# Two loads of chunk 0 become one load in two partition halves, and nine warm-up products become eight

## The chip, the cores and the metric

The kernel runs on one core of one Trainium2 chip. The metric is device time in microseconds (us) of one execution, lower is better. The engines named below are TensorE (PE in rows; its weight loads are PEld), VectorE (DVE), ScalarE (ACT), GpSimd (POOL) and SyncE (SP). Each has its own queue of instructions and waits on semaphores for the others. SP and ACT each also issue DMA transfers on a queue of their own.

## What is computed

A residual layer over 2048 tokens with 512 features: a base projection, and a low-rank addition gated by the two best of eight experts.

```python
base = jnp.einsum('btd,od->bto', x, W)
logits = jnp.einsum('btd,ed->bte', x, Wr) + bias[:, None, :]   # 5.0 at the language's expert
topw, topi = jax.lax.top_k(logits, 2)
gates = jnp.sum(jax.nn.one_hot(topi, E) * jax.nn.softmax(topw)[..., None], axis=-2)
h = jnp.einsum('btd,erd->bter', x, A)
lora_out = jnp.einsum('bter,bte,eor->bto', h, gates, B)
return x + base + 2.0 * lora_out
```

## The kernel before

The 2048 tokens are 16 tiles of 128. The 512 features are four chunks (`k` 0 to 3) of 128, which are the contraction of one product. All weights stand side by side in 648 columns: 392 head columns (`heads_cols`: the second half of W, A and Wr) and 256 base columns (`base_cols`: the first half of W). To keep float32 accuracy in fast products, each operand is split into an upper part (`x_hi`, `w_hi`, a rounded copy) and a lower part (`x_lo`, `w_lo`, what is left), and three products stand for one: hi by hi, hi by lo, lo by hi.

Tiles 0 and 1 come with the weights in one array, `first`, laid out by chunk: 256 columns of x, 4 of language ids, 392 head columns, 256 base columns, 908 in all, on 128 partitions. Before the change they arrive as follows. SP issues x and ids of chunk 0 (L165, semaphore `x_landed`), the base columns of chunk 0 (L166, `wb_landed`), whole chunks 2 and 3 (L168), then tile 2, B and the groups of later tiles. ACT issues the head columns of chunk 0 (L253, `wh_landed`), then whole chunk 1 (L254, `chunk_landed[0]`).

When x has landed, ACT makes `x_hi` of chunk 0 for both tiles (L232), and POOL `x_lo` from it (L211). When the head columns have landed, DVE makes their `w_hi` (L362, `wh_hi_made`), then their `w_lo` (L358). When the base columns have landed, ACT makes their `w_hi` (L235, `w_hi_made`), and DVE their `w_lo`. ACT then goes on with chunk 1.

PE begins with `warm(WARM_UP)`, nine products of ones of 128x512 into a bank that nothing reads (L502). Then, for tiles 0 and 1 of chunk 0 (L429): two head products hi by hi, which wait for `x_hi` and the head columns' `w_hi`; two base products hi by hi, which wait for the base columns' `w_hi`; four products with `x_lo`; two head and two base products with `w_lo`. Chunks 1 to 3 follow in the same manner, then tile 2, and from tile 3 on one step a tile, with the low-rank products of the tile before (L469, L473) and the transposition of its gated heads (L460) in between. No order is planned by a table: it is the order of the code on each engine.

```python
            warm(WARM_UP)
            pe.wait_ge(chunk_hi_made, 1)
            pe.wait_ge(wh_hi_made, 1)
            for t in FIRST:
                heads_product(t, 0, 0)
            pe.wait_ge(w_hi_made, 1)
            for t in FIRST:
                base_product(t, 0, 0)
```

Of the kernel before, what the change touches and what calls it, by code (L numbers as in the profile page):

```python
# [12 lines left out]
P = 128  # L13
# [10 lines left out]
HEADS = REST + ER + E  # L24
SLOTS = 3
LANG_BIAS = 5.0
SCALING = 2.0
WARM_UP = 9
WIDTH = HEADS + BASE


# [1 line left out]
FIRST_X = len(FIRST) * P  # L33
IDS = 4
# [4 lines left out]
def cond_resid_program(nc: bass.Bass, first: bass.AP, xT: bass.AP, x: bass.AP,  # L39
# [11 lines left out]
    with ctx:  # L51
        def sb(name, shape, dt=FP32):
            return ctx.enter_context(nc.sbuf_tensor(name, shape, dt))
# [4 lines left out]
        def sem(name):  # L58
            return ctx.enter_context(nc.semaphore(name))


        first_sb = sb("first_sb", [P, KC, FIRST_X + IDS + WIDTH])
# [31 lines left out]
        warm_ps = ps("warm_ps")  # L94


        x_landed = sem("x_landed")
        xT_third = sem("xT_third")
        xT_group = sem("xT_group")
        x_group = sem("x_group")  # L100
        xT_last = sem("xT_last")
        x_last = sem("x_last")
        wh_landed = sem("wh_landed")
        wb_landed = sem("wb_landed")
        chunk_landed = [sem(f"chunk_landed{k}") for k in range(1, KC)]
        b_landed = sem("b_landed")
# [37 lines left out]
        heads_cols, base_cols, all_cols = slice(0, HEADS), slice(HEADS, WIDTH), slice(0, WIDTH)  # L144
# [4 lines left out]
        w_sb = first_sb[:, :, FIRST_X + IDS:]  # L149
        w = first[:, :, FIRST_X + IDS:]  # L150

        block = ctx.enter_context(nc.Block())

        @block.sync
        def _(sp):
            def load(dst, src, t, n, landed):
                sp.dma_start(dst[:, bass.ds(t, n), :], src[:, bass.ds(t, n), :]).then_inc(landed, 16)

            def store(t, n):
                sp.dma_start(out[:, bass.ds(t, n), :], out_sb[:, bass.ds(t, n), :]).then_inc(out_stored, 16)  # L160

            def load_xT(t, n, landed):
                load(xT_sb, xT, t - len(FIRST), n, landed)

            sp.dma_start(first_sb[:, 0, 0:FIRST_X + IDS], first[:, 0, 0:FIRST_X + IDS]).then_inc(x_landed, 16)  # L165
            sp.dma_start(w_sb[:, 0, base_cols], w[:, 0, base_cols]).then_inc(wb_landed, 16)  # L166
            for k in range(2, KC):
                sp.dma_start(first_sb[:, k, :], first[:, k, :]).then_inc(chunk_landed[k - 1], 16)  # L168
            load_xT(2, 1, xT_third)
            sp.dma_start(b_sb[:, :], b).then_inc(b_landed, 16)  # L170

            load_xT(3, SLOTS, xT_group)
            load(x_sb, x, 0, SLOTS, x_group)
            with sp.Fori(0, GROUPS - 2) as g:
                sp.wait_ge(xT_group, 16 * g + 16)
                sp.wait_ge(x_group, 16 * g + 16)
                load_xT(SLOTS * g + 3 + SLOTS, SLOTS, xT_group)
                load(x_sb, x, SLOTS * g + SLOTS, SLOTS, x_group)
            sp.wait_ge(x_group, 16 * (GROUPS - 1))
            load(x_sb, x, GROUPED - SLOTS, SLOTS, x_group)  # L180
            load_xT(GROUPED, TILES - GROUPED, xT_last)
            load(x_sb, x, GROUPED, TILES - GROUPED, x_last)
            with sp.Fori(0, GROUPS) as g:
                sp.wait_ge(out_made, SLOTS * g + SLOTS)
                store(SLOTS * g, SLOTS)
            for t in range(GROUPED, TILES - 2):
                sp.wait_ge(out_made, t + 1)
                store(t, 1)

            for t in range(TILES - 2, TILES):  # L190
                sp.wait_ge(heads_read, t + 1)
                sp.dma_start(out[:, t, BASE:O], out_sb[:, t, BASE:O]).then_inc(out_stored, 16)
                sp.wait_ge(out_made, t + 1)
                sp.dma_start(out[:, t, 0:BASE], out_sb[:, t, 0:BASE]).then_inc(out_stored, 16)
            sp.wait_ge(out_stored, 16 * (GROUPS + TILES - 2 - GROUPED + 4))
# [33 lines left out]
        @block.scalar  # L229
        def _(act):  # L230
            def chunk_upper(k):
                nc.scalar.activation(x_hi[:, 0:2, chunks[k]], first_x[k], ACT.Copy).then_inc(chunk_hi_made, 1)  # L232

            def w_upper(k, cols):
                nc.scalar.activation(w_hi[:, k, cols], w_sb[:, k, cols], ACT.Copy).then_inc(w_hi_made, 1)  # L235

            def x_upper(t, s, landed, count):

                act.wait_ge(landed, count)
                if not (isinstance(t, int) and t < SLOTS):  # L240
                    act.wait_ge(base_done, t - SLOTS + 1)
                nc.scalar.activation(x_hi[:, s, :], xT_sb[:, t - len(FIRST), :], ACT.Copy).then_inc(x_hi_made, 1)  # L242

            def ghT_upper(t, s, src=ghT_ps):
                act.wait_ge(transposed, t + 1)
                nc.scalar.activation(ghT_hi[s][:, :], src[:, 0:P], ACT.Copy).then_inc(ghT_hi_made, 1)  # L246

            def exponential(t):
                act.wait_ge(top_made, t + 1)
                nc.scalar.activation(e2[:, :], top[:, 0:1], ACT.Exp, scale=-1.0,  # L250
                                     bias=top[:, 1:2]).then_inc(e2_made, 1)

            act.dma_start(w_sb[:, 0, heads_cols], w[:, 0, heads_cols]).then_inc(wh_landed, 16)  # L253
            act.dma_start(first_sb[:, 1, :], first[:, 1, :]).then_inc(chunk_landed[0], 16)  # L254
            act.wait_ge(x_landed, 16)
            chunk_upper(0)
            act.wait_ge(wb_landed, 16)
            w_upper(0, base_cols)
            for k in range(1, KC):
                act.wait_ge(chunk_landed[k - 1], 16)  # L260
                chunk_upper(k)
                w_upper(k, base_cols if k == 1 else all_cols)
            x_upper(2, 2, xT_third, 16)
            act.wait_ge(b_landed, 16)
            nc.scalar.activation(b_hi[:, :], b_sb[:, :], ACT.Copy).then_inc(b_hi_made, 1)
            exponential(0)

            def step(t, j, landed, count):

                x_upper(t + 1, (j + 1) % SLOTS, landed, count)  # L270
                ghT_upper(t - 1, (j - 1) % SLOTS)
                exponential(t)

            exponential(1)
            ghT_upper(0, 0)
            with act.Fori(0, GROUPS - 1) as g:
                for j in range(2, 2 + SLOTS):
                    step(SLOTS * g + j, j, xT_group, 16 * g + 16)
            for t in range(GROUPED - 1, TILES - 1):
                step(t, t, xT_last, 16)  # L280
            last = TILES - 1
            act.wait_ge(x_last, 16)
            act.wait_ge(out_made, last - SLOTS + 1)
            nc.scalar.activation(base_ps[last % SLOTS][:, 0:BASE], x_sb[:, last, 0:BASE],
                                 ACT.Copy).then_inc(last_x_placed, 1)
            exponential(last)
            ghT_upper(last - 1, (last - 1) % SLOTS)
            ghT_upper(last, last % SLOTS, warm_ps)

        @block.vector  # L290
        def _(dve):
# [69 lines left out]
            def heads_upper(k):  # L361
                nc.vector.tensor_copy(w_hi[:, k, heads_cols], w_sb[:, k, heads_cols]).then_inc(wh_hi_made, 1)  # L362

            dve.wait_ge(wh_landed, 16)
            heads_upper(0)
            dve.wait_ge(wh_hi_made, 1)
            w_lower(0, heads_cols)
            dve.wait_ge(w_hi_made, 1)
            w_lower(0, base_cols)
            dve.wait_ge(expert_made, 1)  # L370
            dve.wait_ge(x_landed, 16)
            nc.vector.tensor_scalar(bias[:, :], expert[:, :], ids_sb, LANG_BIAS, ALU.is_equal,
                                    ALU.mult).then_inc(bias_made, 1)
            dve.wait_ge(chunk_landed[0], 16)
# [49 lines left out]
        def _(pe):  # L424
# [75 lines left out]
            def warm(times):  # L500
                for _ in range(times):
                    nc.tensor.matmul(warm_ps[:, :], ones, ones_moving, start=True, stop=True)  # L502

            warm(WARM_UP)
            pe.wait_ge(chunk_hi_made, 1)
# [122 lines left out]
```

## Time and profile before

| | us |
|---|---|
| median of three runs | 80.04 (79.7 to 80.2) |
| the profiled execution's own time | 79.61 |
| its span | 77.8 |

| engine | busy us | share of the span |
|---|---|---|
| PE | 74.0 | 95% |
| PEld | 70.3 | 90% |
| DVE | 48.9 | 63% |
| POOL | 22.6 | 29% |
| ACT | 22.4 | 29% |

A span runs from the first to the last instruction that the profile shows; 79.61 - 77.8 = 1.8 us of the profiled execution lie around it. Busy time of PE counts each product with its modelled end, so that products overlap, and a busy PE is not one at its peak: the distance from one start to the next is the better measure of a product's price. A DMA has two times: that of its issue on a queue, and that of its landing, which is when an engine that waits for it can go on.

### The profile page before, as it was taken

Reading aid. Unit: us, or ns where it says so; the run is one execution under the profiler, and the core shown is the slowest. Engines: PE = TensorE matmul, PEld = TensorE weight load, DVE = VectorE, ACT = ScalarE, POOL = GpSimd, SP = SyncE. Lnnn points to the kernel's source line nnn. Section 1 sums busy time; section 2 is a strip of 40 time slices with the busy share of each in tenths; the row PEclk is TensorE's granted clock in tenths of the full one; section 3 lists DMA queues with packets and bytes.
Section 4 is the critical chain, followed back from the end, with each engine's and each line's share of the span. In section 5 each row is a group of like instructions: output and inputs, shape, how many; then the busy total and the mean of one; then the engine's idle time right before and its main releaser. Section 6 shows DMA issues by size and latency. Waiting matters only on the chain.

```text
span 77.8 us, 1631 instructions
## 1 busy us (share of the span) xinstructions
PE 74.0 (95%) x505; PEld 70.3 (90%) x505; DVE 48.9 (63%) x220; ACT 22.4 (29%) x57; POOL 22.6 (29%) x26
## 2 busy tenths in 40 slices
PE   5979999999999999999999999999999999999960
PEld 2349999899999999999999999999999999999950
DVE  0098958879854829283755739283855739787750
ACT  1647901523503314140504113140404023122100
POOL 4039542055160505123060605123060606000000
PEclk9999999999999999999999999999999999999999
DMA  0999991795597399989900000450000072032143
GB/s 10 308 406 401 419 430 60 167 420 230 83 417 313 54 365 440 383 241 402 388 25 0 0 0 0 177 227 0 0 0 0 0 297 107 0 135 95 44 139 135
DMA packets 3893, 14.24 MB, mean 183 GB/s; under 512 B 432, under 2 KB 1328, under 8 KB 3632
## 3 DMA queue, kind: packets, MB, share of 16 engines
q1 hardware_dynamic: 3600, 13.52, 46.8%
q10 hardware_dynamic: 288, 0.67, 2.2%
q8 instruction: 2, 0.03, 0.2%
q14 instruction: 3, 0.02, 0.1%
HBM read 9.99 MB, written 4.19 MB: 182 GB/s over the span
## 4 chain that ended last, share of the span: by engine, by line
PE 90%; DMA 5%; DVE 1%; ACT 1%; SPq 0%; issue 0%
PE heads_ps L429 43%; PE base_ps L429 28%; PE heads_ps L469 5%; PE base_ps L469 5%; DMA first_sb<-in_first 5%; PE base_ps L473 2%; PE heads_ps L473 2%; PE ghT_ps L460 2%; PE base_ps L453 2%; DVE out_sb L421 1%; ACT w_hi L235 1%; SPq L165 0%; PE warm_ps L460 0%
## 5 line engine op out<-in xcount | busy, mean ns | idle before, releaser
L207 POOL TENSOR_TENSOR x_lo<-xT_sb,x_hi 128x512 fp32r<-128x512 f32 x14 | 18.1, 1294 | 39.0 <-ACT x_hi L242 37.2
L429 PE MATMUL heads_ps<-w_hi,x_hi 128*128 128x392 f32 x64 | 22.2, 357 | 0.0
L429 PE MATMUL heads_ps<-w_hi,x_lo 128*128 128x392 f32 x64 | 21.1, 342 | 0.0
L429 PE MATMUL heads_ps<-w_lo,x_hi 128*128 128x392 f32 x64 | 21.1, 340 | 0.0
L429 PE MATMUL base_ps<-w_hi,x_hi 128*128 128x256 f32 x60 | 16.5, 285 | 0.4 <-ACT w_hi L235 0.4
L429 PE MATMUL base_ps<-w_hi,x_lo 128*128 128x256 f32 x60 | 16.7, 281 | 0.0
L429 PE MATMUL base_ps<-w_lo,x_hi 128*128 128x256 f32 x60 | 16.3, 281 | 0.0
L294 DVE TENSOR_TENSOR ghT_lo<-ghT_ps,ghT_hi 128x128 fp32r<-128x128 f32 x15 | 4.3, 290 | 14.9 <-ACT ghT_hi L246 14.8
L246 ACT ACTIVATE ghT_hi<-ghT_ps 128x128 fp32r<-128x128 f32 x15 | 4.1, 275 | 29.5 <-PE ghT_ps L460 29.5
L429 PEld LDWEIGHTS heads_ps<-w_hi,x_hi 128*128 128x128 f32 x64 | 11.7, 188 | 0.9 <-ACT x_hi L232 0.5
L429 PEld LDWEIGHTS base_ps<-w_hi,x_hi 128*128 128x128 f32 x60 | 11.2, 188 | 0.8 <-ACT w_hi L235 0.8
L429 PEld LDWEIGHTS heads_ps<-w_lo,x_hi 128*128 128x128 f32 x64 | 11.9, 189 | 0.0
L429 PEld LDWEIGHTS heads_ps<-w_hi,x_lo 128*128 128x128 f32 x64 | 11.8, 188 | 0.0
L429 PEld LDWEIGHTS base_ps<-w_lo,x_hi 128*128 128x128 f32 x60 | 11.3, 189 | 0.0
L429 PEld LDWEIGHTS base_ps<-w_hi,x_lo 128*128 128x128 f32 x60 | 11.3, 188 | 0.0
L250 ACT ACTIVATE e<-top 128x1 f32<-128x1 f32 x16 | 4.7, 297 | 15.9 <-DVE top L305 15.9
L242 ACT ACTIVATE x_hi<-xT_sb 128x512 fp32r (+1 forms) x14 | 8.7, 621 | 0.4 <-issue 0.4
L339 DVE TENSOR_TENSOR out_sb<-heads_ps,x_sb 128x256 f32 (+1 forms) x16 | 6.7, 418 | 1.1 <-PE heads_ps L473 1.1
L329 DVE SCALAR_TENSOR_TENSOR gh<-heads_ps,rden,gate 128x128 f32<-128x128 f32 x16 | 5.6, 351 | 1.7
L344 DVE TENSOR_TENSOR out_sb<-base_ps,x_sb 128x256 f32 (+1 forms) x15 | 6.2, 414 | 0.0
L358 DVE TENSOR_TENSOR w_lo<-first_sb,w_hi 128x392 fp32r<-128x392 f32 (+1 forms) x8 | 5.3, 698 | 0.4 <-ACT w_hi L235 0.2
L211 POOL TENSOR_TENSOR x_lo<-first_sb,x_hi 128x256 fp32r<-128x256 f32 (+1 forms) x5 | 3.7, 751 | 4.0 <-ACT x_hi L232 4.0
(51 smaller groups left out, 98.1 us busy)
## 6 DMA issues: line engine op xcount, KB each, us to landing
x_sb<-in_x SPq DMA_DIRECT2D x4, 768.0 KB, 5.6
out<-out_sb SPq DMA_DIRECT2D x4, 768.0 KB, 4.4
xT_sb<-in_xT SPq DMA_DIRECT2D x3, 768.0 KB, 4.3
xT_sb<-in_xT SPq DMA_DIRECT2D x1, 1024.0 KB, 6.3
x_sb<-in_x SPq DMA_DIRECT2D x1, 1024.0 KB, 9.8
first_sb<-in_first SPq DMA_DIRECT2D x2, 454.0 KB, 5.3
out<-out_sb SPq DMA_DIRECT2D x2, 256.0 KB, 2.0
out<-out_sb SPq DMA_DIRECT2D x4, 128.0 KB, 1.7
```

The source lines that it names most:

```text
L207: nc.gpsimd.tensor_tensor(x_lo[:, s, :], xT_sb[:, t - len(FIRST), :], x_hi[:, s, :].bitcast(FP32), ALU.subtract).then_inc(x_lo_made, 1)
L211: nc.gpsimd.tensor_tensor(x_lo[:, tiles, chunks[k]], first_x[k][:, tiles, :], x_hi[:, tiles, chunks[k]].bitcast(FP32), ALU.subtract).then_ ...
L242: nc.scalar.activation(x_hi[:, s, :], xT_sb[:, t - len(FIRST), :], ACT.Copy).then_inc(x_hi_made, 1)
L246: nc.scalar.activation(ghT_hi[s][:, :], src[:, 0:P], ACT.Copy).then_inc(ghT_hi_made, 1)
L250: nc.scalar.activation(e2[:, :], top[:, 0:1], ACT.Exp, scale=-1.0, bias=top[:, 1:2]).then_inc(e2_made, 1)
L294: nc.vector.tensor_tensor(ghT_lo[s][:, :], src[:, 0:P], ghT_hi[s][:, :].bitcast(FP32), ALU.subtract).then_inc(ghT_lo_made, 1)
L329: nc.vector.scalar_tensor_tensor(gh[s][:, :].rearrange("p (e r) -> p e r", r=R), heads_ps[s][:, REST:REST + ER].rearrange("p (e r) -> p e ...
L339: nc.vector.tensor_tensor(out_sb[:, t, BASE:O], heads_ps[s][:, 0:REST], x_sb[:, t, BASE:O], ALU.add).then_inc(heads_read, 1)
L344: nc.vector.tensor_tensor(out_sb[:, t, 0:BASE], base_ps[s][:, 0:BASE], x_sb[:, t, 0:BASE], ALU.add).then_inc(out_made, 1)
L358: nc.vector.tensor_tensor(w_lo[:, k, cols], w_sb[:, k, cols], w_hi[:, k, cols].bitcast(FP32), ALU.subtract).then_inc(w_lo_made, 1)
L429: return nc.tensor.matmul(dst, xs[:, s, chunks[k]], ws[:, k, cols], start=(k == 0 and n == 0), stop=(k == KC - 1 and n == last_n))
L469: nc.tensor.matmul(dst, ghT_hi[s][:, :], bs[:, cols], start=False, stop=False, skip_group_check=True)
```

## The change

The two loads of chunk 0 that the first head products need, x with ids (260 columns) and the head columns (392), become one region of 652 columns. SP asks for it on partitions 0 to 63, ACT on partitions 64 to 127. Both add to one semaphore, `first_landed`, and whoever waited for x or for the head columns waits for 32 on it, so for both halves. The base columns stay a load of their own behind SP's half. One warm-up product is taken out.

```diff
-WARM_UP = 9
+WARM_UP = 8
...
+        ahead_of = FIRST_X + IDS + HEADS
...
-            sp.dma_start(first_sb[:, 0, 0:FIRST_X + IDS], first[:, 0, 0:FIRST_X + IDS]).then_inc(x_landed, 16)
+            sp.dma_start(first_sb[0:P // 2, 0, 0:ahead_of], first[0:P // 2, 0, 0:ahead_of]).then_inc(first_landed, 16)
             sp.dma_start(w_sb[:, 0, base_cols], w[:, 0, base_cols]).then_inc(wb_landed, 16)
...
-            act.dma_start(w_sb[:, 0, heads_cols], w[:, 0, heads_cols]).then_inc(wh_landed, 16)
+            act.dma_start(first_sb[P // 2:P, 0, 0:ahead_of], first[P // 2:P, 0, 0:ahead_of]).then_inc(first_landed, 16)
             act.dma_start(first_sb[:, 1, :], first[:, 1, :]).then_inc(chunk_landed[0], 16)
-            act.wait_ge(x_landed, 16)
+            act.wait_ge(first_landed, 32)
             chunk_upper(0)
...
-            dve.wait_ge(wh_landed, 16)
+            dve.wait_ge(first_landed, 32)
             heads_upper(0)
...
-            dve.wait_ge(x_landed, 16)
+            dve.wait_ge(first_landed, 32)
```

On SP's queue the first loads stand as follows, in the kernel before and then in the changed one (lines of the changed kernel are one higher; `first_sb` is the tile in the core's memory, `in_first` the array in HBM).

```order
L165 DMA first_sb<-in_first 128x260
L166 DMA first_sb<-in_first 128x256
L168 DMA first_sb<-in_first 128x908 x2
L157 DMA xT_sb<-in_xT 128x512
L170 DMA b_sb<-in_b 128x512
```

```order
L166 DMA first_sb<-in_first 64x652
L167 DMA first_sb<-in_first 128x256
L169 DMA first_sb<-in_first 128x908 x2
L158 DMA xT_sb<-in_xT 128x512
L171 DMA b_sb<-in_b 128x512
```

Only the first one changes: 128 rows of 260 columns become 64 rows of 652, and what is asked for before the base columns grows from 130 to 163 KB. ACT's program begins as follows, before and then changed, with the semaphores that each instruction waits for.

```order
L253 DMA first_sb<-in_first 128x392
L254 DMA first_sb<-in_first 128x908
L232 ACT_TABLE_LOAD
L232 ACTIVATE x_hi<-first_sb 128x2x128 [waits x_landed]
L235 ACTIVATE w_hi<-first_sb 128x256 [waits wb_landed]
```

```order
L254 DMA first_sb<-in_first 64x652
L255 DMA first_sb<-in_first 128x908
L233 ACT_TABLE_LOAD
L233 ACTIVATE x_hi<-first_sb 128x2x128 [waits first_landed]
L236 ACTIVATE w_hi<-first_sb 128x256 [waits wb_landed]
```

Here the load ahead of chunk 1 shrinks from 196 to 163 KB, and `x_hi` now waits for both queues' halves instead of SP's load alone. Nothing else changes its place on any engine.

## Rows read from the trace of the kernel before

**Rows 1.** Waits of PE over the whole span: engine, line, releaser: total us, times, longest.

```profile
PE warm_ps L502 <- PEq L621: 0.8, 1, 0.8
PE base_ps L429 <- ACT w_hi L235: 0.4, 1, 0.4
```

**Rows 2.** The chain that ended last, its start and end: start us, us, what.

```profile
0.75 0.39 SPq L165
1.19 3.62 DMA first_sb<-in_first
4.83 0.42 ACT w_hi L235
...
74.86 0.36 PE base_ps L453 x3
...
75.24 0.42 DVE out_sb L421
```

**Rows 3.** DMA issues: engine, count, KB each, median us from issue to landing.

```profile
first_sb<-in_first ACTq DMA_DIRECT2D x1, 454.0 KB, 4.2
first_sb<-in_first ACTq DMA_DIRECT2D x1, 196.0 KB, 3.0
first_sb<-in_first SPq DMA_DIRECT2D x1, 130.0 KB, 2.8
first_sb<-in_first SPq DMA_DIRECT2D x1, 128.0 KB, 3.6
```

**Rows 4.** Timeline of the start: start us, us, engine, line, out<-in, [idle before <-releaser].

```profile
0.75 0.42 ACTq L253 DMA_DIRECT2D first_sb<-in_first  x1
2.87 0.15 PEld L502 LDWEIGHTS warm_ps<-const-bfloat16-1.0 128*128 128x128 bf16 x1 [0.28 <-issue]
3.30 0.15 PEld L502 LDWEIGHTS warm_ps<-const-bfloat16-1.0 128*128 128x128 bf16 x1 [0.28 <-issue]
3.57 0.42 ACT L232 ACTIVATE x_hi<-first_sb 128x256 fp32r<-128x256 f32 x1 [0.61 <-DMA first_sb<-in_first]
3.70 0.10 PEld L502 LDWEIGHTS warm_ps<-const-bfloat16-1.0 128*128 128x128 bf16 x1 [0.25 <-issue]
3.77 0.36 DVE L362 CAST w_hi<-first_sb 128x392 fp32r<-128x392 f32 x1 [3.77 <-DMA first_sb<-in_first]
3.92 0.38 PE L502 MATMUL warm_ps<-const-bfloat16-1.0 128*128 128x512 bf16 x1
4.28 0.60 PE L429 MATMUL heads_ps<-w_hi,x_hi 128*128 128x392 f32 x2
4.83 0.42 ACT L235 ACTIVATE w_hi<-first_sb 128x256 fp32r<-128x256 f32 x1 [0.85 <-DMA first_sb<-in_first]
5.30 0.51 PE L429 MATMUL base_ps<-w_hi,x_hi 128*128 128x256 f32 x2 [0.42 <-ACT w_hi L235]
```

**Rows 5.** Timeline, the inputs of the products behind the first base products.

```profile
4.07 0.73 POOL L211 TENSOR_TENSOR x_lo<-first_sb,x_hi 128x256 fp32r<-128x256 f32 x1 [2.67 <-ACT x_hi L232]
4.17 1.54 DVE L358 TENSOR_TENSOR w_lo<-first_sb,w_hi 128x392 fp32r<-128x392 f32 x2
5.45 0.42 ACT L232 ACTIVATE x_hi<-first_sb 128x256 fp32r<-128x256 f32 x1 [0.20 <-DMA first_sb<-in_first]
5.64 0.34 PE L429 MATMUL heads_ps<-w_hi,x_lo 128*128 128x392 f32 x1
5.76 0.36 DVE L362 CAST w_hi<-first_sb 128x392 fp32r<-128x392 f32 x1
6.59 0.40 PE L429 MATMUL base_ps<-w_lo,x_hi 128*128 128x256 f32 x2
6.83 0.52 PE L429 MATMUL heads_ps<-w_hi,x_hi 128*128 128x392 f32 x2
```

**Rows 6.** Stretches of the start: busy us by engine, PE clock, DMA share, GB/s (last).

```profile
1.60:2.40 0.80, 0.80 (x3) 0.29 (x2) 0.00 (x0) 0.72 (x1) 0.00 (x0) 1.00 0.66 112
4.00:5.00 1.00, 0.88 (x4) 0.30 (x2) 0.97 (x2) 0.17 (x1) 0.73 (x1) 1.00 1.02 404
```

More of the change, by code:

```diff
@@ L94, in cond_resid_program @@
         warm_ps = ps("warm_ps")
-        x_landed = sem("x_landed")
+        first_landed = sem("first_landed")
         xT_third = sem("xT_third")
@@ L102, in cond_resid_program @@
         x_last = sem("x_last")
-        wh_landed = sem("wh_landed")
         wb_landed = sem("wb_landed")
```

## The prediction

> **What bounds the kernel now.** I read the waits of PE first, since PE is busy 95% of the span. In the whole execution PE is shown waiting twice: 0.8 us for the program's start, and 0.4 us for ACT's `w_hi` of the base columns [rows 1]. From 5.30 us on it never waits again. The chain that ended last says the same from the other side: an issue on SP, 3.62 us of a DMA into `first_sb` (the base columns, issued at 1.19, landed at 4.81), 0.42 us of ACT, then PE from 5.30 until 74.86 + 0.36 = 75.22, and one copy of 0.42 us [rows 2]. So the end of the kernel is the start of the first base products plus a constant, as long as nothing behind them comes late. Whatever the change does to the start, only what it does to that 5.30 counts.
>
> The timeline of the start shows which input was last there. `x_hi` starts at 3.57, when x has landed, and ends at 3.99. The cast of the head columns starts at 3.77 and ends at 4.13. The last warm-up product ends at 3.92 + 0.38 = 4.30 as modelled, and the head products start at 4.28; they end at 4.88. Then PE is idle for 0.42 us, until `w_hi` of the base columns, which ACT made from 4.83 to 5.25; ACT itself had stood idle 0.85 us for their DMA [rows 4].
>
> **The change part by part.** *Warm-up, nine to eight.* The first products are 0.43 us apart (weight loads at 2.87 and 3.30), for 512 columns each: that is 1.2 GHz, although the profile prints a granted clock of 1.00 in this stretch. The last ones are closer, the ninth starts at 3.92, 0.22 us after the load at 3.70: 2.4 GHz [rows 4]. Without it PE could go on at 3.92 instead of 3.92 + 0.22 = 4.14. The head products could start when the cast is done, about 4.13 plus the 0.05 us that it takes from `w_hi`'s end at 5.25 to the base products at 5.30: 4.18, so 0.1 us earlier. This lands in the idle 0.42 us before 5.30 and is worth nothing. In an execution in which the clock rises later, nine products take 9 x 0.43 = 3.87 us, to 4.65, and two head products behind them, at half speed about 2 x 392/512 x 0.43 = 0.66 us, end at 5.31: level with the base columns. So the ninth product costs nothing there either.
>
> *First halves instead of x and heads.* Before, 130 KB on SP land 2.8 us after their issue at 0.75, 196 KB on ACT 3.0 us after theirs at 0.75, so at 3.55 and 3.75 [rows 2 to 4]. After, it is 163 KB on each. The sum of 326 KB is the same, on queues that share the bandwidth, and the two should end closer together: I put `first_landed` at 3.6, between the two old ones, so that `x_hi` starts 0.05 us later and the cast 0.15 us earlier. `x_hi` would end at about 4.02 and the cast at 3.96. The head products then start at about 4.1, 0.2 us earlier, and end at 4.7, and PE waits the longer for the base columns. Worth nothing again, and the cover is as before ACT's wait for the base columns. Without that cover it would be worth 0.2 us.
>
> *The base columns.* They are the term that counts, and the trace of before doesn't show them behind this load, so I bound it from both sides. Late end: the two queues get equal shares of bytes. Before, 130 + 128 = 258 KB stood on SP up to the base columns' end; now it is 163 + 128 = 291 KB. The 33 KB more pass together with 33 KB of ACT's, 66 KB at 404 GB/s [rows 6]: 0.17 us later. Early end: between 1.6 and 2.4 us the DMA moved only 112 x 0.8 = 90 KB, at a busy share of 0.66, where 404 GB/s would have moved 323 KB: 233 KB less, so 0.58 us are lost to the beginning [rows 6]. In this stretch the 128 short rows of x and the 128 of the head columns are under way. The change halves their number (64 + 64 rows of 652 columns) for the same bytes; if the loss goes by rows, half of it comes back: 0.29 us earlier. If the loss is one delay at the start, whatever the rows, nothing comes back. Between the ends, +0.17 and -0.29, I take -0.1: the queues before were not served by bytes alone, since 196 KB landed only 0.2 us behind 130 KB, which looks like turns by row rather than by byte, and then the larger share on SP costs less than 0.17.
>
> *The sum.* 0 (warm-up) + 0 (head products) - 0.1 (base columns) = -0.1 us, PE's start of the base products at 5.2. What comes next stands ready: `x_lo` ends at 4.80 and is used at 5.64; `w_lo` of both parts ends at 5.71 and is used by 6.59; `x_hi` of chunk 1 ends at 5.87 and the cast of its heads at 6.12, used at 6.83 [rows 5]. The tightest has 0.7 us. Chunk 1 itself has 33 KB less ahead of it on ACT's queue (163 instead of 196), and had landed when ACT began on it at 5.45 [rows 5]. DVE's and ACT's new waits for both halves have behind them only work on chunk 0, counted above; the second wait on DVE, before `bias`, is long past by then. So 79.61 - 0.1 = 79.5 for the profiled execution. It lies 0.43 us below the median of 80.04; against the median the same step gives 79.94. I say 79.9.
>
> *A rule that speaks against the change.* By the row on landings, two loads on two queues already overlap before the change: 130 and 196 KB land 0.2 us apart [rows 3]. The Trainium skill, DMA: Bandwidth & Descriptors, section Rules for kernel authors, says that two transfers to disjoint partition halves aren't worth it, because both spray over the same 16 engines, and advises one 128-partition transfer. By it the sum would be 0 instead of -0.1. It is a rival below, and the overlap of the two landings agrees with it.
>
> **The rivals.** *No change at all.* The halves move as one load would, the same 326 KB stand ahead of the base columns, and these land at 4.81 as before: 79.6 profiled, 80.0 against the median. For it: the sum of bytes is the same and the queues share the bandwidth. Against it: half as many rows in the stretch in which the DMA runs at 112 GB/s. By the skill's rule named above this is what would happen.
>
> *The base columns land later.* ACT's shorter half lets the 454 KB of chunk 1 start earlier beside them, and SP has 33 KB more ahead. Price 0.05 to 0.17 us, 80.1 to 80.2 against the median. For it: in the chain the base columns take 3.62 us for 128 KB [rows 2], so company matters.
>
> *The larger gain.* If the base columns landed 0.8 us earlier, PE's whole wait of 0.42 us would go and the head products would set the start: with these at 4.1 and 0.37 us for two (two base products take 6.83 - 6.59 = 0.24 us for 256 columns each [rows 5], so 0.24 x 392/256), base products at 4.47, 0.83 us earlier: 79.2 against the median. It needs more than the whole 0.58 us that the start of the DMA loses. Very unlikely.
>
> *Slower, by the clock.* PE works less early: one product fewer, and a wait before the base products of 0.5 instead of 0.42 us. If the clock then stood at 1.2 instead of 2.4 GHz from 5.2 to 7.2, the products of these 2 us would do half their work, and the end would be 1.0 us later: 80.9. The point from which this decides (over 0.8 us) is 1.6 us at the lower clock. For it: the warm-up products up to the load at 3.30 ran at 1.2 GHz, so the rise comes only just ahead of the real work. Against it: it had come by 3.92, before the product that is removed began [rows 4].
>
> **How the numbers follow.** Differences of 1%, 0.8 us, are about what a measurement of this kernel tells from none. Chances: base columns earlier by 0.05 to 0.3 us, 0.50 (the forecast); no change, 0.22; later, 0.17; larger gain, 0.05; clock, 0.06. The first three, together 0.89, lie within 1%, from 79.7 to 80.2. The three runs of before spread by 0.5 us, more than any of these terms, so I widen to 79.3 to 80.4. Faster by over 1% is 0.05, slower by over 1% is 0.06, within is 0.89.
>
> **What would show it.** In the changed kernel's timeline: `x_hi` and the cast of the heads start at the same time, near 3.6; the head products near 4.1 instead of 4.28; ACT's `w_hi` of the base columns at 4.73 or so (4.83 says no change, 4.9 to 5.0 says later); the first base products 0.05 us behind its end; PE waits for it 0.4 to 0.6 us, and for nothing else after it. Between 1.6 and 2.4 us the DMA should move more than 90 KB if rows matter. I would be wrong if PE shows a new wait behind 5.3 us, if product starts at 5.3 us and later are at half the old pace, or if the halves land much apart.

## The result: 2% slower, and the profile after

| | before | changed |
|---|---|---|
| median us (range, runs) | 79.89 (79.7 to 80.2, 6) | 81.44 (81.05 to 82.22, 6) |
| profiled execution, us | 79.61 | 82.22 |
| its span, us | 77.8 | 80.4 |

The ratio is 1.021 (95% interval 1.015 to 1.027). The profiled execution of the changed kernel is the longest of its six, so its trace has to explain 2.61 us; the medians lie 1.55 apart. In all that follows, a time is the median of all executions of a kernel, and a ratio compares only the fast ones, those within 1.5% of the kernel's fastest.

These are the waits of PE in the changed kernel, with the columns of [rows 1]:

```profile
PE heads_ps L430 <- ACT x_hi L233: 1.9, 2, 1.4
PE warm_ps L503 <- PEq L622: 0.8, 1, 0.8
PE heads_ps L430 <- POOL x_lo L212: 0.2, 1, 0.2
```

The wait for the base columns is gone. Two for `x_hi` stand in its place, one of 0.5 and one of 1.4 us. The chain that ended last now goes through another DMA than in [rows 2]: chunk 1, issued by ACT at 1.35 and landed 6.90 us later, at 8.25.

```profile
0.75 0.57 ACTq L254
...
1.35 6.90 DMA first_sb<-in_first
...
8.27 0.43 ACT x_hi L233
...
8.77 1.41 POOL x_lo L212 x2
...
10.22 0.44 PE heads_ps L430
```

The DMA issues of the start have [rows 3] as their counterpart:

```profile
first_sb<-in_first ACTq DMA_DIRECT2D x1, 454.0 KB, 6.9
first_sb<-in_first SPq DMA_DIRECT2D x1, 163.0 KB, 3.0
first_sb<-in_first ACTq DMA_DIRECT2D x1, 163.0 KB, 3.6
first_sb<-in_first SPq DMA_DIRECT2D x1, 128.0 KB, 3.3
```

The timeline is to be read beside [rows 4, 5]:

```profile
0.74 0.56 SPq L166 DMA_DIRECT2D first_sb<-in_first  x1
1.35 0.85 ACTq L255 DMA_DIRECT2D first_sb<-in_first  x1
1.36 0.56 SPq L167 DMA_DIRECT2D first_sb<-in_first  x1
1.97 0.90 SPq L169 DMA_DIRECT2D first_sb<-in_first  x2
4.35 0.42 ACT L233 ACTIVATE x_hi<-first_sb 128x256 fp32r<-128x256 f32 x1 [0.84 <-DMA first_sb<-in_first]
4.87 0.64 PE L430 MATMUL heads_ps<-w_hi,x_hi 128*128 128x392 f32 x2 [0.51 <-ACT x_hi L233]
5.34 0.40 PE L430 MATMUL base_ps<-w_hi,x_hi 128*128 128x256 f32 x2
5.97 0.45 PE L430 MATMUL heads_ps<-w_hi,x_lo 128*128 128x392 f32 x1 [0.23 <-POOL x_lo L212]
8.78 0.42 PE L430 MATMUL heads_ps<-w_hi,x_hi 128*128 128x392 f32 x1 [1.35 <-ACT x_hi L233]
11.20 0.52 PE L430 MATMUL heads_ps<-w_hi,x_hi 128*128 128x392 f32 x2
```

Read against before: the first two issues of each queue take 0.56 to 0.85 us, where they took 0.39 to 0.46. The head products start 0.59 us later (4.87 for 4.28), the base products only 0.04 later (5.34 for 5.30), the products with `x_lo` 0.33 later. Then chunk 1's products start 1.95 us later (8.78 for 6.83). Chunk 2's start at 11.20, where this row of before has 8.62:

```profile
8.62 0.52 PE L429 MATMUL heads_ps<-w_hi,x_hi 128*128 128x392 f32 x2
```

That is 2.58 us, the whole loss: chunk 1's products also take 0.6 us more, since they start the moment its `x_hi` is there and wait for each `x_lo` of POOL (1.41 us for two). Behind it PE runs as before.

The DMA queues from 5 to 9 us show what chunk 1 waited in. q10 is ACT's queue and q1 is SP's; the columns are packets, MB and share. The first two lines are of before, the other two of the changed kernel:

```profile
q1 hardware_dynamic: 592, 1.65, 104.0%
q10 hardware_dynamic: 1, 0.00, 0.0%
```

```profile
q1 hardware_dynamic: 512, 1.33, 92.2%
q10 hardware_dynamic: 49, 0.13, 8.4%
```

Before, one packet of ACT's queue is left at 5 us. In the changed kernel 49 are left, the tail of chunk 1. They are served in small numbers, 31, 14 and 4 in the three microseconds from 5 to 8, beside 512 packets of SP's queue from 5 to 9, which were asked for later.

### The profile page after: what moved, and what is told of

Its sections match the earlier page's. It is cut to its first block, busy times and chain, and to the rows that moved or that the text cites. A ratio compares the mean times of both kernels' runs of the same rounds, so it can differ in the third digit from the quotient of the medians.

```text
span 80.4 us, 1629 instructions
## 1 busy us (share of the span) xinstructions
PE 74.9 (93%) x504; PEld 70.5 (88%) x504; DVE 49.2 (61%) x220; ACT 22.1 (27%) x57; POOL 23.3 (29%) x26
## 4 chain that ended last, share of the span: by engine, by line
PE 84%; DMA 9%; POOL 2%; ACTq 1%; ACT 1%; DVE 1%; issue 0%
PE heads_ps L430 41%; PE base_ps L430 25%; DMA first_sb<-in_first 9%; PE heads_ps L470 5%; PE base_ps L470 5%; PE base_ps L474 2%; PE heads_ps L474 2%; PE ghT_ps L461 2%; PE base_ps L454 2%; POOL x_lo L212 2%; ACTq L254 1%; ACT x_hi L233 1%; DVE out_sb L422 1%; PE warm_ps L461 0%
## 5 line engine op out<-in xcount | busy, mean ns | idle before, releaser
L212 POOL TENSOR_TENSOR x_lo<-first_sb,x_hi 128x256 fp32r<-128x256 f32 (+1 forms) x5 | 4.4, 895 | 6.3 <-ACT x_hi L233 6.3
```

The source lines that it names most:

```text
L212: nc.gpsimd.tensor_tensor(x_lo[:, tiles, chunks[k]], first_x[k][:, tiles, :], x_hi[:, tiles, chunks[k]].bitcast(FP32), ALU.subtract).then_ ...
```

## The experiments

Each kernel was timed beside the kernel before on the same chip, whose medians lay at 79.63 to 79.87. The expectations call the possible causes theories and give each a letter.

**Parts undone.** The warm-up alone, either way (`WARM_UP`, one line):

> The changed kernel with nine warm-up products again. The trace of the change shows PE waiting 0.5 us for x_hi of chunk 0 and 1.4 us for x_hi of chunk 1, both for DMA landings. Theory H (the half-height loads of 64 partitions disturb the transfers): the ninth product lies inside the first wait, so 81.4 as the change, within 0.2. Theory T (only the turns of the two queues changed): the same, 81.4. Theory W (the missing warm-up product costs time through the clock): 80 to 80.5.

It took 81.44 (80.5 to 82.5), ratio 1.012 (1.004 to 1.020), so the ninth product does not undo the loss. Chunk 1 landed at 1.35 + 6.2 = 7.55, and PE waited 0.8 us in all for `x_hi`. This trace, of an 81.51, also accounts for a loss near that of the median: the products of chunk 2 start at 10.52 instead of 8.62, 1.90 us later, and 81.51 - 79.61 = 1.90.

> The kernel before with eight warm-up products, loads untouched. Theories H and T: same as before, 79.9 within 0.2, since PE waits for the base columns anyway. Theory W: 80.5 to 81.5, slower by about what the change was slower.

It took 79.70, ratio 0.998 (0.995 to 1.001), which is no change. But one of eleven executions took 81.95, and it is the one with the trace. Chunk 1 was not late there (1.19 + 4.3 = 5.5); the base columns landed at 1.18 + 4.1 = 5.28, 0.5 us later than before. And its products are slow:

```profile
5.79 0.79 PE L429 MATMUL base_ps<-w_hi,x_hi 128*128 128x256 f32 x2 [0.54 <-ACT w_hi L235]
6.38 0.53 PE L429 MATMUL heads_ps<-w_hi,x_lo 128*128 128x392 f32 x1
6.71 0.41 PE L429 MATMUL base_ps<-w_hi,x_lo 128*128 128x256 f32 x1
```

It is 0.33 us from a head product of 392 columns to the next product, which is 1.2 GHz; before it was 0.18. It stayed so until 9.6 us. So the clock rival exists, but in one execution of eleven, and it explains nothing of a median.

**One load, or halves by columns.** In the first kernel SP asks for the whole region and ACT for no half of it. In the second each queue keeps its 163 KB, but takes half of the columns on all partitions:

```diff
-            sp.dma_start(first_sb[0:P // 2, 0, 0:ahead_of], first[0:P // 2, 0, 0:ahead_of]).then_inc(first_landed, 16)
+            sp.dma_start(first_sb[:, 0, 0:ahead_of // 2], first[:, 0, 0:ahead_of // 2]).then_inc(first_landed, 16)
...
-            act.dma_start(first_sb[P // 2:P, 0, 0:ahead_of], first[P // 2:P, 0, 0:ahead_of]).then_inc(first_landed, 16)
+            act.dma_start(first_sb[:, 0, ahead_of // 2:ahead_of], first[:, 0, ahead_of // 2:ahead_of]).then_inc(first_landed, 16)
```

> The changed kernel, but the 652 columns of chunk 0 are one load on all 128 partitions, asked for by SP alone; ACT asks only for chunk 1. Theory H: no half-height load is left, so chunk 1 lands near 5.4 us or earlier (it is first on its queue) and no DMA comes late; chunk 0 shares the bandwidth with chunk 1 and lands near 4.2; 79.8 to 80.5. Theory T (joined rows of 2.6 KB and a different turn-taking make the lateness): chunk 1 or the base columns late by over 1 us as in the change, 81 or more.

It took 81.93, ratio 1.024 (1.020 to 1.028). Chunk 1 came in time (0.75 + 4.7 = 5.45), as theory H said, but the 326 KB took 4.5 us and landed at 5.25, not at 4.2, so that PE waited 1.4 us for the first `x_hi`. The time I gave was wrong. A second loss stands behind this wait: chunk 0's products ran at the lower clock (0.33 us from a head product to the next) and took from 5.75 to 9.12, 3.4 us. Before, they took from 4.28 to 6.83 with a wait of 0.42, so 2.1 us of work. So the late load and the clock have about equal shares in the loss of this kernel.

> The changed kernel with the region of 652 columns divided by columns, not by partitions: each queue asks for 326 columns on all 128 partitions. Bytes on each queue, order, semaphore and waits are those of the change (163 KB each). Theory H: no half-height load, so as before, 79.7 to 80.1, chunk 1 near 5.4. Theory T: 81.4 as the change, chunk 1 near 7 to 8 us.

Its four executions took 80.0, 80.0, 81.5 and 81.6. Its trace, of an 80.0, has chunk 1 at 1.20 + 4.1 = 5.3, and no packet of ACT's queue after 5 us. So the same bytes on the same queues, at full height, make nothing late, and theory T falls. The first head products in it took 0.99 us, where before they took 0.60, and the distance of 0.33 us lasts until 6.26. This, and the two long executions, suggested the clock:

> The region divided by columns (326 on each queue, all 128 partitions) with nine warm-up products. With eight, two executions took 80.0 and two 81.5 to 81.6 us, though no transfer came late in its trace. Theory K (the clock: the shorter the stretch in which PE is busy before the real products, the more often the rise to 2.4 GHz comes late): nearly all executions at 80.0 or below, at most one in five over 81. Theory X (something in the joined load itself makes some executions long): about half of them at 81.5 again.

It took 79.81 (79.56 to 79.89, 12 runs), ratio 0.998 (0.996 to 1.001). None was long, and in its trace the same head products take 0.60 us. So the ninth product, which I had priced at nothing, may matter here. Two of four against none of twelve is little, though, and neither long execution has a trace. Nine products are no guarantee of an early rise either: the head products take 0.84 us with 32 to 96 partitions, and 0.97 with chunk 1 on SP's queue, both with nine. Joining and balancing as such gain nothing.

These are the head products with eight warm-up products, then with nine (columns), then with nine (chunk 1 on SP):

```profile
4.32 0.99 PE L430 MATMUL heads_ps<-w_hi,x_hi 128*128 128x392 f32 x2
...
4.30 0.60 PE L430 MATMUL heads_ps<-w_hi,x_hi 128*128 128x392 f32 x2
...
4.35 0.97 PE L428 MATMUL heads_ps<-w_hi,x_hi 128*128 128x392 f32 x2
```

**What of the halves hurts.** Ten warm-up products over the wait:

> The changed kernel (partition halves) with ten warm-up products, which reach to about 4.7 to 5.1 us, so over the wait for the first halves. Theory H (half-height loads make chunk 1 late) without the clock: the late chunk remains, PE waits 0.5 us or more for x_hi of chunk 1, landed at 7.5 or later; 80.5 to 81.5. Theory K alone (the clock explains the whole loss of the change): 80.0 to 80.2, as the kernel before.

It took 82.04, ratio 1.021 (1.014 to 1.029), with chunk 1 at 1.35 + 6.4 = 7.75 and a wait of 0.8 us for its `x_hi`. That is theory H, though its range ended at 81.5; the clock alone, with 80.0 to 80.2, is ruled out.

> The changed kernel with the two halves chosen as even partitions (SP) and odd partitions (ACT) instead of lower and upper ones; sizes, queues, order as in the change, eight warm-up products. Theory H (the number of 64 partitions matters, not which ones): as the change, 81.4, chunk 1 late. Theory N (lower and upper halves meet in the same places of the memory, and spreading helps): first halves land by 3.8, chunk 1 near 5.5, 80.0 to 80.3.

It took 81.56, ratio 1.020 (1.015 to 1.025), with issues of 0.56 us and chunk 1 at 1.35 + 6.9 = 8.25. Which 64 partitions a load takes does not matter for it.

> As the change with nine warm-up products, but the region is divided 32 partitions (SP, 82 KB) to 96 partitions (ACT, 245 KB). If what hurts is any height other than 128, both loads have it: ACT's issue over 0.5 us, chunk 1 at 7 us or later, 81 to 82.5. If it is that each queue has fewer and longer rows, ACT now has 96 rows: a smaller delay, chunk 1 near 6, 80 to 80.8.

It took 79.93, ratio 1.003 (1.000 to 1.006), which is neither expectation. The issues took 0.43 and 0.40 us as before, and chunk 1 landed at 1.20 + 4.4 = 5.6. Only `first_landed` was late, with `x_hi` at 4.23.

> As the change with nine warm-up products, divided 48 partitions (SP) to 80 (ACT), nearly even. If a height of 64 is what hurts and no other: issues of 0.40 to 0.45 us, chunk 1 by 5.7, 79.8 to 80.1, as with 32 to 96. If what hurts is an even division (both queues end together, two loads of middle height): issues of 0.5 us or more, chunk 1 at 7 us or later, 80.8 to 81.5.

It took 80.14, ratio 1.006 (1.004 to 1.008), with issues of 0.40 and 0.43 us, chunk 1 at 1.20 + 4.3 = 5.5 and `x_hi` at 4.16. So nearly even parts do little harm; of the heights tried, 64 alone lengthens the issues.

**Where the late chunk comes from.** Three kernels are the kernel before with the head columns in two loads on ACT's queue: first 64 and 64 partitions, then 32 and 96, then 196 and 196 columns at full height.

> The kernel before, nine warm-up products, with one edit: the head columns of chunk 0 are asked for in two half-height loads (64 partitions each), both on ACT's queue; x and the base columns as before, nothing joined. Theory H: half-height loads alone disturb: issues of over 0.5 us on ACT, chunk 1 lands at 7 us or later, its queue still has 20 or more packets after 5 us; 80.5 to 81.5. Theory J (it takes both queues at work on halves, or the joined rows): ACT's queue has one issue more, chunk 1 at 5.5 to 5.9, 79.9 to 80.2.

It took 83.22, ratio 1.045 (1.039 to 1.051), with chunk 1 at 1.97 + 6.9 = 8.87. It looked like theory H, but its time is no evidence on chunk 1. PE waits for the head columns, which landed just before 5.85:

```profile
5.85 0.37 DVE L363 CAST w_hi<-first_sb 128x392 fp32r<-128x392 f32 x1 [5.85 <-DMA first_sb<-in_first]
6.36 0.99 PE L430 MATMUL heads_ps<-w_hi,x_hi 128*128 128x392 f32 x2 [1.58 <-DVE w_hi L363]
...
9.49 0.52 PE L430 MATMUL heads_ps<-w_hi,x_hi 128*128 128x392 f32 x2
```

Chunk 0 then runs at the lower clock, and when chunk 1's products follow at 9.49 their `x_hi` is ready. In the next two kernels the same cast starts at 4.40 and 4.13.

> The kernel before with the head columns in two loads on ACT's queue, of 32 and 96 partitions in place of the 64 and 64 that gave 83.2. The number of loads is the same. If the height of 64 was the cause there: issues of 0.40 to 0.45 us, the head columns near 4.0, chunk 1 near 5.6, 79.8 to 80.2. If one load more on ACT was the cause: 82 to 83.5 again.

It took 82.42, ratio 1.029 (1.025 to 1.033), with chunk 1 at 1.66 + 6.8 = 8.46 and a wait of 1.3 us for it, though the issues took 0.41 to 0.45 us. That speaks for one load more on ACT's queue as the cause.

> The kernel before with the head columns in two loads on ACT's queue, both at full height, 196 columns each. It has the number of loads of the runs with 64 and 64 (83.2) and 32 and 96 (82.4) partitions. If the additional load on ACT's queue is the cause of those: chunk 1 near 8 us, 82 or more. If loads of less than full height are: head columns near 4.0, chunk 1 near 5.7, 79.8 to 80.2.

It took 83.36, ratio 1.042 (1.037 to 1.047), with chunk 1 at 1.67 + 7.3 = 8.97 and a wait of 2.4 us for it. With full height and short issues chunk 1 is as late as ever, so my reading of the first of the three fell. What the three share is the third load, which puts off the issue of chunk 1. Its timeline:

```profile
1.67 0.90 SPq L168 DMA_DIRECT2D first_sb<-in_first  x2
1.67 0.45 ACTq L255 DMA_DIRECT2D first_sb<-in_first  x1
...
9.01 0.42 ACT L232 ACTIVATE x_hi<-first_sb 128x256 fp32r<-128x256 f32 x1 [4.66 <-DMA first_sb<-in_first]
```

SP's chunks 2 and 3 are asked for at the same moment. That gave theory Q, by which they are served ahead of chunk 1. In the next two kernels SP's two loads are made to wait, here for x, and with the halves for SP's own half:

```diff
+            sp.wait_ge(x_landed, 16)
             for k in range(2, KC):
                 sp.dma_start(first_sb[:, k, :], first[:, k, :]).then_inc(chunk_landed[k - 1], 16)
```

> The run with the head columns in two full-height loads on ACT's queue (83.4, chunk 1 landed at 9.0), and SP waits until x has landed (near 3.4 us) before it asks for chunks 2 and 3. Theory Q (chunk 1 is late because SP's two chunks of 454 KB are asked for before or while ACT asks for chunk 1, and are served ahead of it): chunk 1 lands by 5.6, the head columns by 4.0; chunk 2 lands by 7.5; 79.8 to 80.8. If chunk 1 is late for a reason on ACT's own queue: 8 us or more still, 82 or more.

It took 80.92, ratio 1.015 (1.012 to 1.018), so 2.4 us less than without the wait, and 0.1 us above the range expected. ACT's issues are the same, and chunk 1 lands 2.9 us earlier, at 1.68 + 4.4 = 6.08, though not by the 5.6 that was expected:

```profile
1.68 0.45 ACTq L256 DMA_DIRECT2D first_sb<-in_first  x1
...
3.31 0.81 SPq L169 DMA_DIRECT2D first_sb<-in_first  x2
...
6.11 0.42 ACT L233 ACTIVATE x_hi<-first_sb 128x256 fp32r<-128x256 f32 x1 [1.68 <-DMA first_sb<-in_first]
```

What is left of the loss is no longer chunk 1: the head products start at 5.04, chunk 2's products at 9.04 (8.62 before), chunk 3's at 10.97 (10.40 before), and PE later waits 0.6 us for DVE's `gh`, the gated heads.

> The partition halves of the change with nine warm-up products, and SP waits until its own half has landed (near 3.7 us) before it asks for chunks 2 and 3; each half has a semaphore of its own and both are waited for. Theory Q: chunk 1 lands by 6.0 instead of 7.6 to 8.3, ACT's queue has fewer than 10 packets after 5 us, 80.0 to 81.0 (what is left is the late start of the halves, 0.3 us, and chunk 2 later). If the 64-partition loads disturb chunk 1 by themselves: chunk 1 at 7.5 or later, 81.4 or more.

It took 82.82, ratio 1.039 (1.036 to 1.042). As a time it contradicts theory Q; the trace supports it in part. Chunk 1 landed at 1.35 + 5.0 = 6.35 instead of 7.55, where it was with the same nine warm-up products, but not by the 6.0 that was expected, and 41 packets of ACT's queue were left at 5 us where fewer than 10 were expected. With a semaphore for each half, ACT ran its ACT_TABLE_LOAD, which had lain inside the wait before (2.23 to 3.51 in the change), only after the halves had landed:

```profile
4.39 1.28 ACT L235 ACT_TABLE_LOAD   x1 [4.39 <-DMA first_sb<-in_first]
...
5.69 0.42 ACT L235 ACTIVATE x_hi<-first_sb 128x256 fp32r<-128x256 f32 x1
...
7.40 0.53 PE L435 MATMUL heads_ps<-w_hi,x_lo 128*128 128x392 f32 x1
7.73 0.41 PE L435 MATMUL base_ps<-w_hi,x_lo 128*128 128x256 f32 x1
```

`x_hi` is 1.3 us late by that, and the products then run at the lower clock (0.33 us again). My edit put a second cause in, so its time proves nothing.

Last, chunk 1 behind the base columns on SP's queue, with halves and with the full-height loads of before:

> Partition halves as in the change, nine warm-up products, and chunk 1 asked for by SP behind the base columns, so that ACT asks only for its half. Theory H1 (half-height loads delay whatever stands behind them, on either queue): chunk 1 lands at 7 us or later, 80.8 to 81.8. Theory H2 (only two queues that compete behind the halves make one of them late): chunk 1 lands by 6.3, 79.9 to 80.4.

It took 81.28, ratio 1.020 (1.018 to 1.023), with `x_hi` of chunk 1 at 7.19. This is what theory H1 said, that the halves delay what stands behind them on either queue.

> The kernel before, nine warm-up products, all loads at full height, with one edit: chunk 1 moves from ACT's queue to SP's, behind the base columns. It is the comparison for the halves with chunk 1 on SP, and a try at a faster kernel: the base columns no longer share the DMA with chunk 1 and should land near 4.1 instead of 4.81, so PE's wait of 0.4 us for them goes; chunk 1 at 5.3 to 5.6 is still in time for 6.5. 79.4 to 79.6. If the base columns are late for another reason: 79.9.

It took 80.49, ratio 1.007 (1.004 to 1.010), and was uneven (79.6 to 81.1, one at 94.7); 79.4 to 79.6 had been expected. PE's wait for the base columns is gone, but `x_hi` of chunk 1 starts at 6.14 instead of 5.45, and its products are held up by `x_lo`. No version beats the kernel before.

## All traces side by side

The times in this table are worked out from the issue rows of each trace: when ACT's issue of chunk 1 ended, when SP began to issue chunks 2 and 3, and when chunk 1 landed.

| kernel | ACT's issue ends | SP's chunk 2 | chunk 1 lands |
|---|---|---|---|
| before; before with eight | 1.66; 1.65 | 1.66 | 5.4; 5.5 |
| one load | 1.15 | 1.66 | 5.45 |
| column halves, eight and nine | 1.66 | 1.66 | 5.3 |
| 32 to 96; 48 to 80 | 1.65 | 1.67 | 5.6; 5.5 |
| the change; even and odd | 2.20 | 1.97 | 8.25 |
| the change, nine; ten | 2.19 | 1.97 | 7.55; 7.75 |
| three loads on ACT: 64, 64; 32, 96; full | 2.57; 2.11; 2.12 | 1.66 | 8.87; 8.46; 8.97 |
| full, SP waits | 2.13 | 3.31 | 6.08 |
| halves, SP waits | 2.19 | 3.73 | 6.35 |

Chunk 1 landed at 7.55 or later in all seven traces in which SP began on its large loads before ACT's issue of chunk 1 had ended, and by 6.35 in all others of the table. The two runs in which SP waits bring the landing forward by 2.9 and by 1.2 us. So SP's large loads, when they are asked for that early, are shown to cause most of chunk 1's lateness with three loads at full height, and a part of it with the halves. That the end of ACT's issue is the boundary is only what the table suggests: SP's loads were put off by over 1.6 us in both runs, and none moved them by a few tenths. How the queues bring it about is not shown.

It is not all. With SP waiting, chunk 1 behind the halves still lands 0.95 us later than before (6.35 for 5.4), though its issue began only 0.15 us later. With chunk 1 on SP's own queue the halves still cost 7.19 - 6.14 = 1.05 us on it. And any part height delays the first data: `x_hi` starts at 3.8 with column halves, at 4.16 to 4.23 with 48 to 80 and 32 to 96, at 4.07 to 4.50 with 64 and 64. Why a load of 64 partitions takes 0.55 to 0.61 us to issue, and one of 32, 48, 80, 96 or 128 some 0.39 to 0.45, stays open.

## Why the prediction was wrong, point by point

- **That PE's start after the base columns sets the end:** this was right for the kernel before. That the same chain would hold after the change was the mistake. The prediction had named the sign of it, a new wait of PE behind 5.3 us; there is one, of 1.4 us.
- **The base columns, -0.1 us:** they landed at 1.36 + 3.3 = 4.66, 0.15 us earlier than 4.81, inside the bounds of -0.29 to +0.17. It was worth nothing, since the head products had become later and ended behind them. That the size came near was luck. The reason given was that fewer, longer rows would bring back some of the bytes lost at the start, more than 90 KB from 1.6 to 2.4 us. The DMA moved 82 x 0.8 = 66 KB there, at a busy share of 0.40 (columns as in [rows 6]):

```profile
1.60:2.40 0.80, 0.80 (x3) 0.28 (x2) 0.00 (x0) 0.17 (x1) 0.00 (x0) 1.00 0.40 82
```

- **First halves, `first_landed` at 3.6, worth 0:** a term that was mis-sized. It was 4.35, 0.75 us later. I had taken only bytes and turns. The issues, 0.56 us instead of 0.39 and 0.42, are some 0.15 of it. The rest is not explained: with uneven parts the issues were short and `x_hi` still started at 4.16 to 4.23. No row of before had a load of another height than 128, and I put no bound on what such a height costs. PE's start on the products with `x_lo` moved by 0.33 us with it.
- **"What comes next stands ready", chunk 1 with 33 KB less ahead of it:** the step that failed. I gave it 0.7 us of slack and looked only at bytes ahead on its queue. It landed 2.85 us later (8.25 for 5.4), and PE waited 1.4 us for it. Its issue had moved from 1.20 to 1.35 and took 0.85 us, beyond the start of SP's large loads; I had named the second issue of each queue nowhere. With nine warm-up products the landing was 2.15 us late, and putting off SP's loads gave back 1.2 of them. What makes the other 0.95 stays open.
- **The warm-up, 0:** the median agrees (79.70 with eight). I had argued that the rise comes before the ninth product; in the trace of the change all eight are 0.43 us apart, so the rise came later there. With column halves, eight gave two long executions of four and nine none of twelve, so the product may have a price in single executions. The clock, a rival at 0.06, is not the loss of the change: with nine and with ten products the loss stays.
- **The rule on partition halves:** the Trainium skill, DMA: Bandwidth & Descriptors, section Rules for kernel authors, advises against them and says that the halves share the same engines. The advice holds. I took its reason for a price, no change, and that does not: the measured price is 1.55 us, and 0.2 to 0.4 us for uneven parts.
- **The two slower rivals** named the base columns (0.05 to 0.17 us) and the clock (1.0 us). Neither is what happened: it was chunk 1, and no rival priced it.

## What to carry to other kernels

Where several loads start a kernel on two queues, price their issues and the order of these over both queues, not only the bytes on each. A load that is needed early should be asked for before the other queue starts on its large ones; where its issue ended 0.45 to 0.9 us later here, by halves of 64 partitions or by one load more ahead of it, it landed 2.1 to 3.6 us later. Divide by columns at full height rather than into two times 64 partitions. And time a shorter warm-up over many executions, since a few long ones do not show in a median.

## What was not expected of the hardware

- A load of 64 partitions took 0.55 to 0.61 us to issue, and the load behind it on its queue was longer too: 0.85 instead of 0.46 for 454 KB in the change, 0.60 with the head columns in 64 and 64, and 0.56 instead of 0.43 for the base columns. 32, 48, 80 and 96 partitions took 0.40 to 0.45.
- Chunk 1, issued 0.5 us later than in the kernel before at the same size, landed 3.6 us later (8.97 for 5.4), beside loads of the other queue asked for at the same time. With these asked for 1.6 us later it landed at 6.08.
- The profile prints a granted clock of 1.00 in stretches in which it is 0.33 us from the start of a product of 392 columns to the next, so at 1.2 GHz; only the distances of the products show it.
